# Scores made a second time, transposed and with the row maxima added on TensorE, in a decoder layer kernel

## The reference

```
x = layernorm(x + attn(x))     # gated linear recurrence, 512 channels, with an RMS norm and an output product
x = layernorm(x + xattn(x, ctx, ctx))
x = layernorm(x + ffn(x))      # silu(gate) * up, 1024 hidden channels
```

```
qk  = einsum("bdm,bdn->bmn", q, k) * scale     # 256 x 256 scores of each of 8 heads
sm  = softmax(qk, axis=-1)
ret = einsum("bmn,bcn->bcm", sm, v)            # c: the head's 32 rows
```

## Time and profile before

| | us |
|---|---|
| median of 3 runs | 172.75 (172.38 to 174.07) |
| the profiled execution | 172.81 |
| its span, first to last instruction | 171.0 |
| PE busy (share of the span) | 154.1 (90%) |
| DVE busy | 117.2 (69%) |
| ACT busy | 111.9 (65%) |
| POOL busy | 79.6 (47%) |
| mean granted clock of TensorE | 0.969 of full |

### The profile page before, as it was taken

The page is one execution under the profiler, slowest core; times in us unless marked ns, Lnnn a source line. Parts: engine busy times, 40 slices in busy tenths (PEclk is TensorE's granted clock), DMA queues, the critical chain, the costliest instruction groups (busy, mean ns, idle before and its releaser), DMA issues.

```text
span 171.0 us, 4005 instructions
## 1 busy us (share of the span) xinstructions
PE 154.1 (90%) x1528; PEld 142.0 (83%) x1528; DVE 117.2 (69%) x214; ACT 111.9 (65%) x258; POOL 79.6 (47%) x95
## 2 busy tenths in 40 slices
PE   7999784599987999999999999999999999899950
PEld 2799674498985899999799999979999979799940
DVE  2568887945987949786795779849749086536642
ACT  3697999859999878299776764854738860124400
POOL 1219999968975384225067123735100455016301
PEclk9999999569999999999999999999999999999995
DMA  5999960100002200000010000100020000000011
GB/s 162 312 395 402 401 230 7 59 4 0 4 0 61 67 0 4 0 0 4 2 61 4 0 6 0 61 4 0 0 64 1 2 4 0 0 0 4 0 61 61
DMA packets 5138, 10.47 MB, mean 61 GB/s; under 512 B 640, under 2 KB 1664, under 8 KB 5120
## 3 DMA queue, kind: packets, MB, share of 16 engines
q1 hardware_dynamic: 5120, 10.23, 17.1%
HBM read 9.18 MB, written 1.05 MB: 60 GB/s over the span
## 4 chain that ended last, share of the span: by engine, by line
PE 70%; POOL 10%; issue 4%; ACT 4%; DMA 4%; DVE 3%; SPq 2%; POOLq 0%; DVEq 0%; ACTq 0%
PE banks L379 38%; PE banks L523 9%; PE banks L463 7%; PE banks L529 4%; PE banks L485 4%; PE banks L450 4%; DMA ctx_raw<-ctx 4%; ACT numer L631 2%; POOL ctx_h_lo L889 2%; POOL xt_lo L923 1%; POOL w_gate_lo L907 1%; POOL o_lo L914 1%; PE banks L473 1%; PE banks L425 1%; PE banks L495 1%
## 5 line engine op out<-in xcount | busy, mean ns | idle before, releaser
L956 POOL TENSOR_TENSOR g_lo<-gu,g_hi 128x512 fp32r<-128x512 f32 x15 | 19.9, 1337 | 34.4 <-ACT g_hi L673 34.4
L631 ACT ACTIVATE numer<-banks,neg_top 128x256 f32<-128x256 f32 x64 | 29.5, 482 | 6.6 <-DVE neg_top L804 6.4
L804 DVE TENSOR_REDUCE neg_top<-banks 128x4 f32<-128x1024 f32 x16 | 19.1, 1217 | 12.0 <-PE banks L450 12.0
L665 ACT ACTIVATE gu<-banks 128x512 f32<-128x512 f32 x16 | 9.6, 598 | 19.4 <-PE banks L379 18.0
L836 DVE SCALAR_TENSOR_TENSOR gu<-gu,banks 128x512 f32<-128x512 f32 x16 | 10.9, 680 | 13.2 <-ACT gu L665 13.2
L642 ACT ACTIVATE prob<-banks 128x1024 f32<-128x1024 f32 x16 | 15.7, 1022 | 4.5 <-PE banks L463 4.4
L937 POOL TENSOR_SCALAR ve<-mv 128x2 f32<-128x2 f32 x12 | 2.3, 193 | 31.0 <-DVE mv L769 30.9
L523 PE MATMUL banks<-w_down_hi,g_hi 128*128 128x256 f32 x64 | 16.0, 284 | 0.0
L775 DVE TENSOR_SCALAR res<-banks,mv,rstd 128x256 f32<-128x256 f32 x24 | 11.9, 536 | 5.9 <-POOL rstd L939 5.8
L463 PE MATMUL banks<-ident,numer 128*128 128x128 f32 x128 | 15.8, 273 | 0.1
L523 PE MATMUL banks<-w_down_lo,g_hi 128*128 128x256 f32 x64 | 15.7, 279 | 0.0
(11 more groups left out here) (111 smaller groups left out, 456.2 us busy)
## 6 DMA issues: line engine op xcount, KB each, us to landing
prob<-w_ffn SPq DMA_DIRECT2D x4, 512.0 KB, 11.6
res<-xT SPq DMA_DIRECT2D x4, 256.0 KB, 5.5
ctx_raw<-ctx SPq DMA_DIRECT2D x4, 256.0 KB, 6.9
ctx_t<-ctxT SPq DMA_DIRECT2D x4, 256.0 KB, 4.9
res<-x SPq DMA_DIRECT2D x4, 256.0 KB, 6.4
numer<-w_ffn SPq DMA_DIRECT2D x2, 512.0 KB, 9.1
out<-res SPq DMA_DIRECT2D x4, 256.0 KB, 2.1
prob<-w SPq DMA_DIRECT2D x3, 256.0 KB, 4.6
```

The costliest lines, as they stand in the source:

```text
L631: ins = nc.scalar.activation(numer[:, n % 2, 2 * h + c, :], place["scores", b, i][:, 2 * h + c, :], ACT.Exp, bias=neg_top[:, 2 * i + h, c: ...
L665: nc.scalar.activation(gu[:, n % 2, :].rearrange("p (k t) -> p k t", k=2), place["hidden", b, i][:, 0:2, :], ACT.Tanh, scale=0.5).then_inc ...
L804: nc.vector.tensor_reduce(neg_top[:, 2 * i:2 * i + 2, :].rearrange("p h c -> p (h c)"), place["scores", b, i][:, :, :], AX_X, ALU.max, neg ...
L956: nc.gpsimd.tensor_tensor(g[1][:, 2 * i:2 * i + 2, :], gu[:, n % 2, :].rearrange("p (k t) -> p k t", k=2), g[0][:, 2 * i:2 * i + 2, :], AL ...
```

## The change

Four things change in the attention, and one in the layernorms.

- The scores are made twice. The first time, as before, only for the row maxima (`scores` and `maximum`); their banks are free once the maxima are taken. The second time (`shifted`) the operands change places, so that the scores come out with the key axis on the partitions, where context needs them. The maximum then belongs to a column, not to a partition, so it can't be the bias of an ACT instruction.
- So the maxima are added on PE. DVE splits the negated maxima into high and low part, put side by side in 2 of 32 columns that are else zero (`split_top`); PE turns them (`turn_top`: two matmuls of 128 x 128, against the unit matrix in fp32r); ACT copies them to `top_rows` (`keep_top`); and `shifted` ends each group with a product of `pick`, a constant that is 1 in those two rows of each 32 and else 0, with `top_rows`. A step has 32 matmuls in place of 24.
- ACT's exp is one instruction of 128 x 1024 for two heads, straight into `prob`. turn_exp, its copies, and `numer` are gone.
- The denominators come from PE (`sums`): 16 f32 matmuls of 32 columns of ones with `prob`. DVE transposes the result in blocks of 32 x 32, takes reciprocals of 128 x 16, and transposes them, spread over 512 columns, into `inv_b` (`invert`). widen, inverse and their copy are gone.
- The first two layernorms are applied by ACT (Identity with a scale and a bias of each partition) in place of DVE. The bias is minus mean times inverse deviation, for which POOL has two more small instructions (128 x 2) in `norm_root`.

PLAN and BANKS are new throughout. Beside the new steps the orders of all engines differ: on SP ctx of batch 0 is issued before the third load of xT and not behind it, and x of batch 1 much later.

The core of the diff. Lines taken out are left out of it, since they stand in the kernel above (turn_exp, inverse, the old exp, keep_turned, keep_inverse, invert, widen); of PLAN a few keys are shown. What is new in `exp` replaces both the old exp and keep_turned:

```diff
+    "pe.scores": [[31.84, 39.61], [56.16, 68.65], [78.69, 94.69], [111.68, 122.93]],
+    "pe.turn_top": [[36.14, 43.53], [63.04, 72.97], [89.88, 101.13], [118.12, 127.35]],
+    "pe.shifted": [[37.07, 44.48], [66.2, 76.04], [90.82, 104.2], [119.06, 128.28]],
+    "pe.sums": [[48.27], [80.09], [108.07], [132.15]],
+    "pe.context": [[50.07], [81.89], [109.88], [133.96]],
...
+    "act.norm1": [[29.13], [48.83], [64.55], [100.8]],
+    "act.x1": [[30.37], [53.74], [69.56], [107.57]],
+    "act.top": [[36.6, 44.0], [65.73, 73.44], [90.35, 103.25], [118.59, 127.81]],
+    "act.exp": [[38.5, 39.55, 45.99, 47.16], [67.47, 68.52, 77.31, 78.98], [92.09, 93.76, 105.47, 106.52], [120.33, 121.38, 129.55, 130.6]],
+    "act.norm2": [[57.12], [88.94], [116.77], [142.37]],
...
+        top_cols = sb("top_cols", [P, TT, EC, Q, D], F32R)
+        top_rows = sb("top_rows", [P, TT, E], F32R)
...
+        freed_by = {"value": [state_done], "decay": [tan1], "query": [out_done], "scores": [top_done],
+                    "turn_top": [top_kept], "shifted": [exp_done], "hidden": [g_done], "down": [normed[2]], "low": [low_lo],
+                    "squares": [sq_turned], "mixed": [normed[0]], "sums": [sums_turned], "context": [normed[1]],
...
+            def turn_top(b, t):
+                ps = place["turn_top", b, t]
+                pe.wait_ge(const_r, 3)
+                pe.wait_ge(top_lo, TT * b + t + 1)
+                for c in range(EC):
+                    ins = nc.tensor.matmul(ps[:, 0, c * P:(c + 1) * P], top_cols[:, t, c, :, :].rearrange("p j d -> p (j d)"), ident_r[:, :],
+                                           start=(c == 0), stop=True, skip_group_check=True)
+                ins.then_inc(top_turned, 1)
+            def shifted(b, t):
+                slot = b % 2
+                pe.wait_ge(top_kept, TT * b + t + 1)
+                for c in range(EC):
+                    for xn, cn in ((0, 0), (0, 1), (1, 0)):
+                        for j in range(Q):
+                            ps = place["shifted", b, 2 * t + j // 2]
+                            rows = slice(j * D, (j + 1) * D)
+                            nc.tensor.matmul(ps[:, EC * (j % 2) + c, :], ctx_h[cn][rows, slot, t, c * P:(c + 1) * P],
+                                             x1_h[xn][rows, slot, t, :], start=(xn + cn == 0), stop=False)
+                    for j in range(Q):
+                        ps = place["shifted", b, 2 * t + j // 2]
+                        rows = slice(j * D, (j + 1) * D)
+                        ins = nc.tensor.matmul(ps[:, EC * (j % 2) + c, :], pick[rows, :], top_rows[rows, t, :],
+                                               start=False, stop=True)
+                ins.then_inc(shifted_done, 1)
+            def sums(b, i):
+                ps = place["sums", b, i]
+                pe.wait_ge(exp_done, HP * (b + 1))
                 for t in range(TT):
                     for c in range(EC):
+                        for j in range(Q):
+                            ins = nc.tensor.matmul(ps[j * D:(j + 1) * D, t, :], ones[:, :], prob[:, Q * t + j, c, :],
+                                                   start=(c == 0), stop=(c == EC - 1))
+                ins.then_inc(sums_done, 1)
             def context(b, i):
                 ps = place["context", b, i]
+                pe.wait_ge(exp_done, HP * (b + 1))
...
+            def keep_top(b, t):
+                act.wait_ge(top_turned, TT * b + t + 1)
+                if b >= 1:
+                    act.wait_ge(shifted_done, TT * (b - 1) + t + 1)
+                nc.scalar.activation(top_rows[:, t, :], place["turn_top", b, t][:, 0, :], ACT.Copy).then_inc(top_kept, 1)
             def exp(b, i):
...
+                act.wait_ge(shifted_done, TT * b + i // 2 + 1)
                 if b == 0:
                     act.wait_ge(ffn_w_lo, 2 * (i + 3))
                 if b >= 1:
                     act.wait_ge(context_done, b)
+                    act.wait_ge(sums_done, b)
+                nc.scalar.activation(prob[:, 2 * i:2 * i + 2, :, :].rearrange("p h c e -> p (h c) e"), place["shifted", b, i][:, :, :],
+                                     ACT.Exp).then_inc(exp_done, 1)
+            def norm_apply(n, b, tile):
+                act.wait_ge(shift_turned[n], b + 1)
+                for t in range(TT):
+                    ins = nc.scalar.activation(res[:, b, t, :], tile[:, t, :], ACT.Identity, bias=shift[:, n, t:t + 1],
+                                               scale=rstd[:, n, t:t + 1])
+                ins.then_inc(normed[n], 1)
+            def norm1(b, i):
+                norm_apply(0, b, place["mixed", b, 0])
+            def norm2(b, i):
+                norm_apply(1, b, place["context", b, 0])
...
+            dve.wait_ge(consts, 3)
+            nc.vector.tensor_reduce(picked[:, :], ident[:, :].rearrange("p (j d) -> p j d", j=Q)[:, :, 0:2],
+                                    mybir.AxisListType.XY, ALU.add).then_inc(picked_done, 1)
+            dve.wait_ge(picked_done, 1)
+            nc.vector.tensor_copy(pick[:, :], picked[:, :].to_broadcast([P, P])).then_inc(const_r, 1)
...
             def maximum(b, i):
+                t, k = i // 2, i % 2
+                dve.wait_ge(scores_done, TT * b + t + 1)
+                if b >= 1:
+                    dve.wait_ge(top_lo, TT * (b - 1) + t + 1)
+                nc.vector.tensor_reduce(neg_top[:, t, 2 * k:2 * k + 2, :].rearrange("p h c -> p (h c)"), place["scores", b, i][:, :, :],
                                         AX_X, ALU.max, negate=True).then_inc(top_done, 1)
+            def split_top(b, t):
+                whole = neg_top[:, t, :, :].rearrange("p j c -> p c j")
+                dve.wait_ge(top_done, HP * b + 2 * t + 2)
+                if b == 0:
+                    dve.wait_ge(const_r, 3)
+                if b >= 1:
+                    dve.wait_ge(top_turned, TT * (b - 1) + t + 1)
+                nc.vector.tensor_copy(top_cols[:, t, :, :, 0], whole).then_inc(top_hi, 1)
+                dve.wait_ge(top_hi, TT * b + t + 1)
+                nc.vector.tensor_tensor(top_cols[:, t, :, :, 1], whole, top_cols[:, t, :, :, 0], ALU.subtract).then_inc(top_lo, 1)
             def invert(b, i):
+                dve.wait_ge(sums_done, b + 1)
+                nc.vector.transpose(sums_t[:, :, :].rearrange("p k d -> p (k d)"),
+                                    place["sums", b, 0][:, :, :].rearrange("p t n -> p (t n)")).then_inc(sums_turned, 1)
+                dve.wait_ge(sums_turned, b + 1)
+                nc.vector.reciprocal(inv[:, :], sums_t[:, :, 0]).then_inc(inv_done, 1)
+                dve.wait_ge(inv_done, b + 1)
+                nc.vector.transpose(inv_b[:, :, :].rearrange("p t (k d) -> p (t k) d", d=D),
+                                    inv[:, :].unsqueeze(2).to_broadcast([P, TT * H, D])).then_inc(inv_spread, 1)
...
+            nc.gpsimd.memset(top_cols[:, :, :, :, :].bitcast(F32), 0.0).then_inc(const_r, 1)
+            nc.gpsimd.tensor_scalar(ident_r[:, :], ident[:, :], 1.0, 0.0, ALU.mult, ALU.add).then_inc(const_r, 1)
...
+                if n < 2:
+                    pool.wait_ge(rstd_done[n], b + 1)
+                    nc.gpsimd.tensor_tensor(shift[:, n, :], mv[:, n, :, 0], rstd[:, n, :], ALU.mult).then_inc(shift_done[n], 1)
+                    pool.wait_ge(shift_done[n], b + 1)
+                    nc.gpsimd.tensor_scalar(shift[:, n, :], shift[:, n, :], -1.0, 0.0, ALU.mult, ALU.add).then_inc(shift_turned[n], 1)
```

259 lines of the change are left out of this document (97 added, 162 removed).

## The result

The changed kernel takes **180.98 us** (median of 4 runs, 180.19 to 182.42) against 172.8 before (172.38 to 174.07): a ratio of 1.047, 95% interval 1.038 to 1.056. It is slower by 8.2 us. The forecast was 172.3, so it was wrong by 8.7 us and in its sign, and the time lies outside the range (170.0 to 175.3).

A forecast was written before the change was run, and what follows sets the result against it. From 56.8 to 164.65 us PE's work and waits bound the kernel; before 55, ctx's landing and POOL's queue. Lead -3.9, PE work +1.4, waits +2.0 gave -0.5 on 172.81: 172.3 us, range 170.0 to 175.3.

The forecast's parts named there:

- The forecast's own sign of being wrong: End of batch 0's context step: forecast near 51.3 us; an end after 53 would show the prediction wrong.
- the lead of 3.9: Front half, to the end of context(0): 3.9 us gained by earlier ctx and ACT normalising; range 1.5 to 4.5.
- the mark of 55.2: End of context(0) to beat: 56.8 us before, lowered to 55.2 because two PE steps now lie behind it.
- PE's work +1.4: PE-bound half, batches 1 to 3: added minus removed PE steps, +1.4 us; bounds -0.4 to 4.3.
- the new waits of 2.0: Second half: PE waits more often on ACT and DVE, together 2.0 us.
- the price of the split: DVE: eight splits of two tiny instructions, each instruction about 0.2 us, between 0.24 and nothing.
- my own walk: Front-half timeline: scores(0,0) at 31.1 us, POOL's queue from 28.4 to 45.9, sums and context finishing near 50.7.
- The rival of the clock falling in the middle: PE between scores(0,0) and context(0): six microseconds at 1.2 GHz cost three, 175.3 us; decides above 4.4; chance 0.06.
- The waits for down(1)'s bank and for the last scores step: Second half: hidden(2,1) waits 0.5 us for down(1)'s bank; the last scores step's maxima and split leave 0.4.
- my 1.15: PE: length of a shifted step, eight rounds of four matmuls, 1.15 us; bounds 0.91 and 1.21.
- The two moved steps: PE: low(3,0), 0.70 us, and scores(1,0), 0.91 us, moved from ahead of context(0)'s end to behind it.
- The cover of the second half: Between context and turn_x: at least 6.4 us of PE work hides a 4.9 us normalising chain, 1.4 to spare.

The follow-up runs named there:

- experiment 1: Changed kernel without its split: maxima written rounded straight into the columns turn_top reads; 175.13 us median, ratio to the kernel before 1.007.
- experiment 3: Kernel before plus three unread 128x8 DVE instructions (PSUM copy, SBUF copy, SBUF subtraction) beside every second maximum; 175.79 us, one run.
- experiment 5: Changed kernel, split kept, but negated maxima held in PSUM in the scores' bank, which PE rewrites only after the split; 184.14 us, ratio 1.061.
- experiment 8: Changed kernel without the split, plus five, two and five unread PE products ahead of scores(0,0), shifted(0,0) and scores(0,1); 173.91 us, ratio to before 1.005.
- experiment 9: Kernel before with two 32-row matmuls inserted between ordinary products in each of 16 hidden steps; 180.93 us, ratio 1.046.
- experiment 10: Kernel before with one more ordinary 128x256 matmul in each of 16 hidden steps, no shape change; 174.93 us, ratio 1.011.
- experiment 11: Kernel before with two 128x128 products on their own stationary operand, turn_top's form, in 16 hidden steps; 176.27 us, ratio 1.020.
- experiment 7: Changed kernel without the split, plus fourteen, five and nine unread PE products ahead of scores(0,0), shifted(0,0) and scores(0,1); 178.22 us, ratio to before 1.030.

## Why the prediction was wrong

In the profiled execution the last matmul ended 9.9 us after its forecast (174.02 against 164.15): 7.1 of it had arisen when context(0) ended (58.43 against 51.3), 2.7 behind. The forecast's own sign of being wrong, context(0) ending after 53, came. In the terms of the sum, -3.9 + 1.4 + 2.0: the lead of 3.9 became a delay of 3.2 (58.43 against the mark of 55.2), PE's work +1.4 became +3.8, and the new waits of 2.0 were 2.35.

- **The step that failed is the price of the split**: "8 splits of two tiny instructions (about 0.2 each, between the 128x64 transpose's 0.24 and nothing)". The first pair took 1.26 and 1.19, 2.5 us and not 0.4. The median is 0.19, so the price was right for the instruction and wrong for its place. The forecast's upper end came from a row in which DVE reads PSUM. The row that would have told is in the prediction itself: x's remainder, a DVE instruction whose inputs lie in SBUF, "the 0.7 as its other instructions of this size, or the 1.64 that it took here,", beside POOL's remainders. I read the 1.64 as one instruction's mishap and did not ask what POOL was doing. And my own walk had POOL "from 28.4 on" occupied until 45.9, with eleven instructions of 1.27: every split of batch 0 had to fall beside them. Experiments 1, 3 and 5 show this cause: removal, the two forms by themselves, and a change of where the inputs lie, with the wait for the bank that goes with it.

The Trainium skill (SBUF — State Buffer, SBUF: two separate sides) describes a pair of SBUF ports that VectorE and GpSimd share, held for a whole instruction while the other waits; VectorE takes it with two SBUF inputs or in a 2-port mode. The trace agrees where it can be held against it: 1.12 and 1.20 us ending with POOL's instructions, 0.17 with an input from PSUM. That the copy, which has one input, is in such a mode no row shows; it was held up like the subtraction. By that rule each split beside POOL would have been priced at up to two of POOL's instructions, an estimate of 2.5 us by its 1.27, and not at 0.4.

- **The clock.** The rival of the clock falling in the middle is what happened (chance given: 0.06), by another wait than I had named: PE busy 0.97 us from 36 to 40, then 0.50 until 50. It "decides above 4.4 us at the low level"; ten came. In the profiled run shifted(0,0), scores(0,1) and mixed(1) took 2.10, 1.65 and 5.15 instead of 1.15, 0.91 and 2.85, so 4.0 us more. It is a follower of the split's wait in part only: even without the split six of ten runs have a low mean clock and about 2 us more (experiment 1), and filling gave 1.2 (experiment 8). "PE's work there is denser, 4.3 in 7 us" was no argument: it averages over a wait of 1.3 us ahead of scores(0,1).
- **The front as a whole**: the first split 2.0 beyond its price (36.88 to 39.37, less the 0.5 I had), half speed 4.0, the profiled run's own early clock fall 1.2: 7.2, which is what lies between 58.43 and the 51.18 of experiment 8. The start of the walk was wrong too: scores(0,0) stood at 33.40, and at 32.23 in experiment 1 without the early fall, not at 31.1. Half a microsecond of that is x's remainder, 1.18 and not 0.7, another 0.25 ACT's normalising of two tiles, 1.02 and not 0.77.
- **New waits**, forecast 2.0: PE's idle time behind context(0) grew by 2.35, but 1.48 of it is the third slow split (turn_top at 81.97), and 0.56 the last turn_top to shifted pair, for which I had said 0.5. Three waits of 0.10 stand at 89.04 (sums(1), forecast 0.4), 100.17 and 129.60 (shifted behind turn_x, forecast 0.1 each). The waits for down(1)'s bank and for the last scores step did not come. That the sum was nearly right was luck.
- **PE's work**, forecast +1.4, is +3.8: from the mark of 55.2 before and from the end of context(0) after, 109.45 and 115.59 us to the last matmul, less the 2.35 of idle. It doesn't hang on the split: in experiment 8, from 51.18 to 165.2, it is +3.7. The new steps have the forecast's lengths (shifted 51.51 to 52.65, 1.14; sums 1.74 to the next start; turn_top 0.17 to 0.24). What was missed is beside them. I counted 0.19 per visit where experiments 9 and 10 have 0.375: six times 0.19, 1.1 us. "That share is inside my 1.15" is the false sentence. turn_top's successor takes 0.05 more, but with that turn_top costs no more than the 0.25 that it was priced at (0.20 in experiment 11). The two moved steps, with their borders, cost 1.91 and not the 1.61 that the mark allows, 0.3. And the matmuls of down, which the change does not touch, run a little slower: blocks of twelve start 1.43 to 1.44 us apart (168.26, 169.69, 171.13, 172.57), where they started 1.40 to 1.42 apart before (159.02, 160.44, 161.84, 163.24); over the sixteen blocks that is 0.6 us. Why, no run shows. Of the 2.4 us too little 0.4 stays open.

The cover of the second half was also reckoned wrongly: 48 rounds at 0.12 are 5.8 us and not 6.4. It held all the same; PE did not wait for the normalised tile ahead of turn_x.

Right were: ACT's relief, the transposes, the length of each new step, and that the front could be 4 us shorter (experiment 8). The constants and the issue order, put at nothing, no run tests. Wrong by size: ACT's normalising, 0.56 and not 0.38, covered in the second half.

## What to carry to other kernels

Before a small VectorE instruction goes onto a chain, look at where its inputs lie and at what GpSimd runs at that moment: with both in SBUF here it cost what was left of GpSimd's instruction, not its own length. Price a visit to another matmul shape by its two neighbours as well, with a run that adds nothing but the visit. And where PE must wait, its clock is part of the wait's price: filling an idle stretch with products cut to its length made the kernel before 0.9% faster, and filling that was too long made experiment 7 1.8% slower than experiment 1.
